# A fused attention and int8 feed-forward kernel: softmax normalised in the PSUM banks, and the attention product in goes of two key tiles

## What is computed

```python
q, k, v = x @ Wq, x @ Wk, x @ Wv            # heads of 32; each k/v head serves 4 query heads
scores = einsum('bhqd,bhkd->bhqk', q, k) / sqrt(32)
out = einsum('bhqk,bhkd->bhqd', softmax(scores), v) @ Wo
x = layernorm(x + out)
x_q, w_q = int8 rows of x and of weight, each scaled by its row's largest magnitude / 127
y = (x_q @ w_q.T) * x_scale * w_scale + bias
x = layernorm(x + y)
```

## Time and profile before

| | us |
|---|---|
| median of 3 runs (lowest, highest) | 860.35 (858.87, 862.44) |
| the profiled execution: its own time | 858.5 |
| its span, first to last instruction | 856.7 |
| PE, DVE, ACT, POOL busy | 774.4, 698.3, 494.5, 607.6 |
| one middle batch (batch 5, 549.9 to 648.1 holds its most part) | 98.3 |

### The profile page before, as it was taken

How to read it: one execution, slowest core, us unless ns; L and a number is a source line. 1 busy time by engine, 2 the same in 40 slices (tenths; PEclk the granted TensorE clock), 3 DMA queues, 4 the chain that set the end, 5 groups by cost and what they waited for, 6 DMA issues and landing times.

```text
span 856.7 us, 12297 instructions
## 1 busy us (share of the span) xinstructions
PE 774.4 (90%) x3752; PEld 431.5 (50%) x3752; DVE 698.3 (82%) x1131; ACT 494.5 (58%) x904; POOL 607.6 (71%) x673
## 2 busy tenths in 40 slices
PE   7698999899899998999899998999899998899874
PEld 5444554465456644565445654566445653344441
DVE  4689668789987898888988898878988789779667
ACT  3155566565566656666556556656666645556644
POOL 3365487687785878767876797957877877678935
PEclk9889899999999999999999999999999998889995
DMA  7531123042132223232231322322230421300001
GB/s 217 136 116 38 39 60 96 20 112 63 51 112 50 66 72 98 52 79 83 63 100 41 84 63 60 102 60 78 73 102 27 112 63 50 99 26 26 26 25 49
DMA packets 40897, 61.89 MB, mean 72 GB/s; under 512 B 10385, under 2 KB 12433, under 8 KB 40833
## 3 DMA queue, kind: packets, MB, share of 16 engines
q1 hardware_dynamic: 39488, 57.38, 24.3%
q0 software_dynamic: 1344, 3.74, 1.6%
HBM read 20.71 MB, written 8.39 MB: 34 GB/s over the span
## 4 chain that ended last, share of the span: by engine, by line
PE 48%; DVE 18%; issue 15%; POOL 12%; POOLq 3%; ACT 3%; DMA 1%; SPq 0%; DVEq 0%; ACTq 0%
POOL prob_sum L1007 10%; PE front_bank L328 9%; PE s_bank L373 8%; PE st_bank L382 8%; PE o_bank L397 8%; DVE row_max L786 7%; PE tail_bank L328 6%; DVE o_norm L810 3%; PE z_bank L411 2%; POOLq L1016 2%; PE front_bank L335 1%; DVE o_norm L804 1%; ACT probs L612 1%; PE tail_bank L462 1%; DVE one_ish L799 1%
## 5 line engine op out<-in xcount | busy, mean ns | idle before, releaser
L786 DVE TENSOR_REDUCE row_max<-s_bank 128x1 f32<-128x512 f32 x512 | 339.9, 681 | 84.7 <-PE s_bank L373 82.7
L612 ACT ACTIVATE probs<-st_bank 128x512 f32<-128x512 f32 x512 | 293.4, 595 | 190.7 <-PE st_bank L382 183.7
L1007 POOL TENSOR_TENSOR prob_sum<-prob_sum,probs 128x512 f32<-128x512 f32 x248 | 344.2, 1418 | 6.5 <-ACT probs L612 6.3
L382 PE MATMUL st_bank<-q_stack,k_stack 98*128 98x512 f32 x512 | 231.7, 454 | 9.9 <-ACT probs L612 6.2
L373 PE MATMUL s_bank<-k_stack,q_stack 96*128 96x512 f32 x512 | 214.2, 421 | 24.8 <-DVE row_max L786 23.4
L1007 POOL TENSOR_TENSOR prob_sum<-probs 128x512 f32<-128x512 f32 x128 | 170.3, 1356 | 66.7 <-PE z_bank L411 48.0
L382 PEld LDWEIGHTS st_bank<-q_stack,k_stack 98*128 98x128 f32 x512 | 98.5, 193 | 117.2 <-ACT probs L612 77.2
L397 PE MATMUL o_bank<-probs,v_tok 128*32 128x512 f32 x1024 | 143.1, 632 | 0.7 <-ACT probs L612 0.7
L373 PEld LDWEIGHTS s_bank<-k_stack,q_stack 96*128 96x128 f32 x512 | 99.8, 195 | 65.8 <-DVE row_max L786 35.4
L1012 POOL TENSOR_TENSOR rs<-mv,small 128x1 f32<-128x1 f32 x64 | 12.7, 198 | 124.4 <-DVE mv L830 124.4
L328 PE MATMUL tail_bank<-wo_hi,o_hi 128*128 128x512 f32 x112 | 45.9, 410 | 6.5 <-issue 6.5
(11 more groups left out here) (193 smaller groups left out, 1041.2 us busy)
## 6 DMA issues: line engine op xcount, KB each, us to landing
q_stack<-q_parts SPq DMA_DIRECT2D x357, 64.0 KB, 2.0
x_tok<-in_L_attn_x SPq DMA_DIRECT2D x36, 256.0 KB, 3.8
y_sb<-in_L_attn_x SPq DMA_DIRECT2D x28, 256.0 KB, 2.8
out<-u_sb SPq DMA_DIRECT2D x28, 256.0 KB, 2.3
k_stack<-k_parts SPq DMA_DIRECT2D x90, 64.0 KB, 2.0
probs<-in_L_attn_Wq SPq DMA_DIRECT2D x1, 1024.0 KB, 8.3
o_norm<-in_L_attn_Wo POOLq DMA_DIRECT2D x4, 256.0 KB, 7.6
q_stack<-neg_max SPq DMA_DIRECT2D x64, 8.0 KB, 1.8
```

The lines of the kernel that those rows point to most:

```text
L382: nc.tensor.matmul(st_bank[:, j % 2, :], k_stack[0:STACK_M, p, j, kt * P:(kt + 1) * P], q_stack[0:STACK_M, i, j, :], start=True, stop=True ...
L612: nc.scalar.activation(probs[:, kt, j, :], st_bank[:, j % 2, :], ACT.Exp, scale=SCALE).then_inc(exp_done, 1)
L786: nc.vector.tensor_reduce(row_max[:, i % 2, j * QT + qt:j * QT + qt + 1], s_bank[:, qt % 2, :], AX_X, ALU.max).then_inc(max_done, 1)
L1007: nc.gpsimd.tensor_tensor(prob_sum[:, j, :], first, probs[:, kt, j, :], ALU.add).then_inc(sum_done, 1)
```

## The change

1. `o_evacuate` and the tile `one_ish` go. `scale_o` reads `o_bank` itself, and `pv` of the next group waits for `scaled_done` instead of `o_read`.
2. `correct` writes `-z * inv` back into `z_bank`, and `normalize` reads it there. So `max_t` now waits for `norm_done` instead of `correct_done`.
3. `rescale` writes `tail_bank` in place, `residual2` reads it there. The bank is freed by `z2_done` instead of `u_done`. The wait for the store moves to `normalize2` on ACT.
4. `pv` runs for two steps in a row, at slots 5, 13, 21, ... 61 (step n and n + 1 at slot 4n + 13), instead of one step at slots 1, 5, 9, ...
5. All three tables have new numbers. Some of `MIDDLE` are shown; `FIRST` and `LAST` move in like manner.

```diff
-PV_AT = 1
+PV_STEPS, PV_LAG = 2, 13
...
-    sums_pe=(7, 23, 37, 52),
-    inv_act=(7, 24, 38, 53),
-    correct_dve=(9, 25, 40, 54),
-    scale_dve=(9, 26, 43, 55),
-    norm_dve=(11, 33, 44, 59),
-    o_act=(3, 17, 36, 52),
-    max_pe=(10, 27, 42, 55),
+    sums_pe=(7, 23, 39, 55),
+    inv_act=(7, 23, 39, 55),
+    correct_dve=(8, 23, 39, 56),
+    scale_dve=(9, 24, 40, 57),
+    norm_dve=(10, 25, 41, 58),
+    max_pe=(12, 27, 43, 60),
...
                 if kt == 0:
-                    wait(pe, o_read, b * GROUPS + i)
+                    wait(pe, scaled_done, b * GROUPS + i)
...
             def max_t(b, i):
-                wait(pe, correct_done, b * GROUPS + i - 1)
+                wait(pe, norm_done, b * GROUPS + i - 1)
...
                 if part == 0:
-                    pe.wait_ge(u_done, FREE + b * QT + t)
+                    pe.wait_ge(z2_done, FREE + b * QT + t)
...
-                    if j == PV_AT and s > 0:
-                        pv(b, p, s - 1)
-                    if j == PV_AT and s == 0 and tail:
-                        pv(b - 1, 1 - p, STEPS - 1)
+                    for first in range(0, STEPS, PV_STEPS):
+                        for n in range(first, first + PV_STEPS):
+                            if u == first * NKV + PV_LAG:
+                                pv(b, p, n)
+                            if u + UNITS == first * NKV + PV_LAG and tail:
+                                pv(b - 1, 1 - p, n)
...
-            def o_evacuate(b, p, i):
-                act.wait_ge(pv_done, b * STEPS + (i + 1) * QT)
-                nc.scalar.mul(o_norm[:, p, i, :], o_bank, -1.0).then_inc(o_read, 1)
...
             def normalize2(b, t):
                 w = buffers(b, t)
                 act.wait_ge(rs2_done, b * QT + t + 1)
+                if not is_last(b):
+                    act.wait_ge(out_stored, FREE + (b * QT + t) * 16)
...
                 dve.wait_ge(inv_done, b * GROUPS + i + 1)
                 wait(dve, norm_done, b * GROUPS + i)
-                nc.vector.tensor_tensor(one_ish[:], z_bank, inv_sum[:], ALU.mult).then_inc(correct_done, 1)
+                nc.vector.scalar_tensor_tensor(out=z_bank, in0=z_bank, scalar=-1.0, in1=inv_sum[:], op0=ALU.mult,
+                                               op1=ALU.mult).then_inc(correct_done, 1)
...
             def scale_o(b, p, i):
-                dve.wait_ge(o_read, b * GROUPS + i + 1)
+                dve.wait_ge(pv_done, b * STEPS + (i + 1) * QT)
                 dve.wait_ge(inv_done, b * GROUPS + i + 1)
-                nc.vector.tensor_tensor(o_norm[:, p, i, :], o_norm[:, p, i, :], inv_sum[:], ALU.mult).then_inc(scaled_done, 1)
+                nc.vector.tensor_tensor(o_norm[:, p, i, :], o_bank, inv_sum[:], ALU.mult).then_inc(scaled_done, 1)
...
-                nc.vector.scalar_tensor_tensor(out=o_norm[:, p, i, :], in0=one_ish[:], scalar=2.0, in1=o_norm[:, p, i, :],
-                                               op0=ALU.subtract, op1=ALU.mult).then_inc(norm_done, 1)
+                nc.vector.scalar_tensor_tensor(out=o_norm[:, p, i, :], in0=z_bank, scalar=2.0, in1=o_norm[:, p, i, :],
+                                               op0=ALU.add, op1=ALU.mult).then_inc(norm_done, 1)
...
-                if not is_last(b):
-                    dve.wait_ge(out_stored, FREE + n * 16)
-                nc.vector.scalar_tensor_tensor(out=w["u"], in0=w["bank"], scalar=x_scale[:, t, 1:2],
+                nc.vector.scalar_tensor_tensor(out=w["bank"], in0=w["bank"], scalar=x_scale[:, t, 1:2],
                                                in1=w_scale[:], op0=ALU.mult, op1=ALU.mult).then_inc(u_done, 1)
...
-                nc.vector.tensor_tensor(w["z"], w["u"], w["z"], ALU.add).then_inc(z2_done, 1)
+                nc.vector.tensor_tensor(w["z"], w["bank"], w["z"], ALU.add).then_inc(z2_done, 1)
```

More of the change, by code:

```diff
@@ L542, in _ @@
             segment(B - 1, 1, front=False, tail=True)
-            pv(B - 1, 1, STEPS - 1)
+            for first in range(0, STEPS, PV_STEPS):
+                for n in range(first, first + PV_STEPS):
+                    if first * NKV + PV_LAG >= UNITS:
+                        pv(B - 1, 1, n)
             sums(B - 1, GROUPS - 1)
```

150 lines of the change are left out of this document (71 added, 79 removed).

## The result

| | before | changed |
|---|---|---|
| median of 4 runs (lowest, highest), us | 860.5 (858.9, 862.4) | 892.5 (886.7, 911.9) |
| ratio, with its 95% interval | | 1.035 (1.028 to 1.042) |
| the profiled execution, its span | 858.5, 856.7 | 895.5, 893.7 |
| middle batches 1 to 6, us | 99.5, 98.8, 98.3, 98.5, 98.3, 102.8 | 106.9, 106.2, 106.0, 99.8, 107.1, 106.3 |
| batch 0, batch 7 | 94.6, 88.4 | 94.1, 87.7 |

The kernel is 3.5% slower; 832.5 us was forecast. The six middle batches lost 36 us, the rest nothing to speak of.

What follows compares the result with a forecast made beforehand. PE was taken to bound some 70 us of each 98 us batch and DVE the other 28. Six middle batches at -3.8 us and two ends at -2.5 gave -27.8, so 832.5 us as the median (chance 0.50), range 808 to 850.

Steps and rivals of the forecast that it cites:

- only half comes through: Rival: other waits replace DVE's long operations, the DVE part halves to -1.9 us a batch; 846 us, chance 0.22.
- The slower case: Rival: DVE is held at `correct` in every group, 2.2 us for 32 groups; 893 us, chance 0.09.
- The price of PSUM: With PSUM sources, `normalize` and `correct` take 0.74 us, `scale_o` and `residual2` 0.68; a PSUM write costs no more.
- -3.8 forecast: Sum for a middle batch: -3.2 - 0.9 - 1.9 + 0.6 + 1.2 + 0.4 = -3.8 us, times six.
- the 3.2 us of that term: DVE-bound end of a batch, slots 46 to 63: four long DVE operations get shorter, saving 3.2 us a batch.
- The first wait: PE's 1.09 us wait behind `normalize` and the splits, ahead of the output projection: 0.9 us saved a batch.
- (a): `max_t` for the next batch moves from slot 55 to 60, its chain ends later: costs 0.6 us, between 0 and 2.5.
- (d): Bank freed by `residual2` instead of `rescale`, 0.7 us later, with `out_proj` two slots behind: costs nothing.
- (b): `correct` stands closer behind `sums`, at slots 8, 23, 39 and 56, with row maxima queued behind it: costs 1.2 us a batch.
- (c): The last feed-forward product follows its transposes in slot 59, so PE waits for ACT: costs 0.4 us a batch.
- The forecasts for batches 0 and 7: End batches: three `scale_o`, three `normalize` and the pairs in batch 0, fewer pairs in batch 7; -2.5 us each.

Runs made afterwards that it cites:

- the run with POOL's wait: The changed kernel with POOL waiting, before the seventh add of a batch's first group, for DVE's `o_split_lo` of tile 0: 857.2 us, ratio 0.997.

## Why the prediction was wrong

**The step that failed.** In the rival "only half comes through" I wrote that `o_split_lo` keeps both sources in SBUF, and took it to keep its price. The median of all cases was 1.16 us and the longest 1.84, so its term was nothing. It became 7.6 us in five batches and 4.9 in a sixth, with what PE lost behind it 33 to 37 us. I priced the operations that the change takes away from where POOL holds them, and not the one that stays. No row of before has such a case: POOL's run of seven adds beside that slot could have been read there, but with it stood a price of 1.80 us, and the 7.6 could not be read.

**892.5 is the time of the wrong rival.** The slower case said 893 us, by DVE held at `correct` for 1.3 us or more in every group. The trace has 17.7 us over 32 groups there, 0.55 each. The mechanism is not that one.

**The price of PSUM: right.** 0.70, 0.68, 0.68, 0.75 and 0.69 us, with no spread to speak of, for a forecast of 0.74 and 0.68. DVE's write into a bank costs nothing to speak of (0.75 against 0.74 for `rescale`). The Trainium skill's 120 cycles for a PSUM source against 58 (VectorE: DVE Perf Modes, section "The TRN2 errata — SBUF-src ops pay a fixed extra latency per instruction") is not seen: `scale_o` with a PSUM source takes 681 ns, and 681 was its median from SBUF. The prediction found 51 ns between the quickest `normalize` and the quickest `rescale` and took it for the bank's; with a bank as its source `normalize` still takes 681, so it was not.

**A middle batch: -3.8 forecast, -2.1 at best.** The batches with neither stall nor fallen clock are the cleanest measure: 96.2 us in the run with POOL's wait, where batches 3 to 5 of before took 98.3 to 98.5. Its windows (batches 2 and 3):

```profile
242.20:338.40 96.20, 90.89 (x464) 53.12 (x464) 79.51 (x138) 58.00 (x108) 70.90 (x80) 1.00 0.27 75
338.40:439.10 100.70, 95.39 (x465) 54.40 (x465) 79.67 (x138) 58.07 (x108) 70.84 (x80) 0.95 0.27 72
```

DVE's busy time fell by 4.7 us (84.2 in batch 3 of before), the batch by 2.1. The 28 us at its end, where DVE is the limit, did get shorter, slots 48 to 63 from 22.1 to 21.2 us; but of the 3.2 us of that term not a third arrived. The first wait (1.09 at slot 14) went, as forecast, and new ones of 0.76, 0.19 and 0.43 us came ahead of slots 2 and 10 and in slot 12. A pair takes 1.85 us from its start to the next score, as the prediction had it; but where PE is the limit (slots 16 to 47, four pairs, 1.3 us forecast) only 0.4 us came through, new waits of 0.53 and 0.62 us at slots 45 and 46 among what took the rest. (a) is nothing: at slot 0 of these batches PE does not wait.

The lists of PE's waits over the whole span say where the rest went. Before:

```profile
PE z_bank L419 <- DVE row_max L786: 10.4, 7, 1.6
PE st_bank L382 <- ACT probs L612: 6.2, 13, 1.3
PE tail_bank L462 <- ACT xq_sb L660: 1.1, 2, 0.9
```

With the change and POOL's wait:

```profile
PE s_bank L360 <- DVE row_max L768: 14.5, 32, 0.8
PE st_bank L369 <- ACT probs L606: 20.7, 37, 1.1
PE tail_bank L451 <- ACT xq_sb L645: 6.6, 15, 1.1
PE tail_bank L315 <- DVE z_sb L853: 3.9, 8, 1.4
```

The waits for DVE's row maxima fell from 33.8 us (23.4 of them) to some 15, as the prediction had it. Those for ACT rose from 7.3 to 27.3 us. The prediction looked at ACT's busy time, found it the limit nowhere and gave it no term; but PE waits for the one exp that is next, and other jobs of ACT stand in front of it. In batch 2 of that run these are the two operations of `inverse` (1.23 us) ahead of PE's wait of 0.78 us at slot 58, and `normalize2`, which had itself waited 2.17 us for POOL, ahead of the 0.76 at slot 2. The last line is (d), the bank freed by `residual2`: put at nothing, it is 3.9 us.

**The clock was in no term.** In the same run batch 3 is 4.5 us longer than batch 2 with the same work: its granted clock is 0.95, PE's two levels in turn, where batch 2 has 1.00. The falls cost 1.7 us in slots 0 to 15 and 2.8 in slots 48 to 63. What brings one is not shown: the waits ahead of the second fall are the same in batch 2, and batch 5 of before kept 1.00 through waits of 1.09, 1.06 and 1.59 us. Six batches of 96.2 us in place of those of the profiled run (595.0 us together) would be 18 us less.

**(b) had the wrong sign, (c) was a swap.** I charged 1.2 us a batch for `correct` right behind `sums`; undoing it, with `max_t` where it is, costs 4 us a batch, since `max_t` now needs `norm_done`. I had that in part 2 of the change and did not follow it to slots 27, 43 and 60. (c), 0.4 a batch, measured 1.3 us over the whole kernel, within the noise of the two runs.

**The sum itself.** I added parts at the places of before. In the places of the changed kernel the pairs are worth 64 us and the normalisation 55, and together with those places, POOL's wait and (c) undone they make 4. So the new places lean on both parts and would be dear without them; a kernel with the new tables and neither part was not run, so their own cost stays unmeasured. The forecasts for batches 0 and 7, -2.5 each, measured -0.4 and -0.7.

## What to carry to other kernels

When a change speeds up the operations of DVE that share SBUF operands with a busy POOL, list the ones that stay, and look for a place where POOL has several instructions ready in a row: one wait of POOL on DVE's result there cost 0.7 us a batch and saved some 33 in all. A batch that is a ring of queues does not give back what single terms promise: a wait removed at one slot turned up at another three times here, and waits taken off behind DVE came back behind ACT, an engine that is busy for little over half the time. Some of PE's waits, not all, were paid again in half clock behind them. Follow a new wait condition (`norm_done` for `correct_done`) at every slot where its instruction stands, and test parts in the places that they were made for.
